# Group 0's lags and the warm-up on all rows, the count tables in step 6, and a new order of the front and the first step

## The reference, cut to what matters

```
ctx    = causal_ema(x, tau_ctx)
gated  = x * sigmoid([x, ctx] @ Wg.T + bg)
h1     = gelu(x @ Wn1.T + bn1)
mod    = 0.5 + sigmoid(h1 @ Wn2.T + bn2)              # 32 values per token
traces = causal_ema(gated * mod[d], tau[d])           # for each of the 32 d
temporal = sum_d traces[d] * softmax(blend)[d]
out    = (gelu(x @ Wsoma.T + bsoma) * sigmoid(temporal @ Wtemp.T + btemp)) @ Wout.T
x      = x + layernorm(out) * gamma + beta

lam    = 10 * exp(-5 * u_prev);   use_sparse = lam >= 1        # per batch
dense  = softmax(q k.T / sqrt(8) + lam * (prior_mask - 1)) v
sparse = softmax over the 32 listed keys of each query, v of the same keys
x      = x + where(use_sparse, sparse, dense) @ Wo.T + bo
```

## Time and profile before

| | us |
|---|---|
| median of three runs (lowest to highest) | 340.48 (339.88 to 341.51) |
| the profiled execution | 342.68 |
| its span in the trace | 340.8 |
| PE busy in the span | 318.4 (93%) |
| DVE | 277.4 (81%) |
| POOL | 246.3 (72%) |
| ACT | 214.9 (63%) |

### The profile page before, as it was taken

The page is one execution under the profiler, slowest core; times in us unless marked ns, Lnnn a source line. Parts: engine busy times, 40 slices in busy tenths (PEclk is TensorE's granted clock), DMA queues, the critical chain, the costliest instruction groups (busy, mean ns, idle before and its releaser), DMA issues. The chain is left out here.

```text
span 340.8 us, 10005 instructions
## 1 busy us (share of the span) xinstructions
PE 318.4 (93%) x3333; PEld 212.4 (62%) x3333; DVE 277.4 (81%) x1453; ACT 214.9 (63%) x458; POOL 246.3 (72%) x298
## 2 busy tenths in 40 slices
PE   7998889999999999989987799999999999999995
PEld 2545355574746556565534576778878777878873
DVE  3895579897888789596788857899999999999982
ACT  5760225555555655644625788788888888888863
POOL 3154266768588676545536777799999999999990
PEclk9996799999999999997999999999999999999999
DMA  6600002023130603210551144565444345401011
GB/s 193 193 3 0 31 0 65 31 68 73 41 100 2 126 14 80 62 32 11 81 82 18 36 90 87 83 109 138 126 102 127 91 127 94 89 4 33 3 33 33
DMA packets 29154, 23.07 MB, mean 68 GB/s; under 512 B 2736, under 2 KB 27824, under 8 KB 29104
## 3 DMA queue, kind: packets, MB, share of 16 engines
q1 hardware_dynamic: 29104, 22.44, 29.0%
HBM read 7.75 MB, written 2.10 MB: 29 GB/s over the span
## 5 line engine op out<-in xcount | busy, mean ns | idle before, releaser
L1593 POOL TENSOR_TENSOR arena<-arena,neg_max 128x512 f32<-128x512 f32 x128 | 129.7, 1042 | 14.0 <-DVE neg_max L1435 13.5
L1435 DVE CUSTOM_DVE_ANT_0 arena<-ps,arena 128x128 f32<-128x128 f32 x512 | 113.7, 286 | 11.2 <-PE ps L765 5.5
L1080 ACT ACTIVATE arena<-ps 128x512 f32<-128x512 f32 x128 | 69.5, 596 | 9.1 <-PE ps L779 9.0
L779 PE MATMUL ps<-ident_sb,arena 128*128 128x128 f32 x512 | 68.2, 276 | 0.0
L1512 POOL TENSOR_TENSOR arena<-arena 128x448 f32<-128x448 f32 (+6 forms) x56 | 42.4, 757 | 31.2 <-DVE arena L1270 27.8
L779 PEld LDWEIGHTS ps<-ident_sb,arena 128*128 128x128 f32 x512 | 56.4, 141 | 7.0 <-issue 4.7
L1435 DVE DVE_READ_ACCUMULATOR2_ANT neg_max<- 128x1 f32 x512 | 42.4, 83 | 0.1
L795 PE MATMUL ps<-arena 128*32 128x128 f32 x1024 | 41.2, 279 | 0.0
L1499 POOL TENSOR_TENSOR arena<-decay_a,arena 128x192 f32<-128x192 f32 x32 | 19.4, 635 | 25.3 <-ACT arena L924 25.3
L1270 DVE SCALAR_TENSOR_TENSOR arena<-ps,lag_c,arena 128x448 f32<-128x448 f32 (+6 forms) x56 | 25.8, 484 | 8.5 <-POOL arena L1512 6.6
L795 PEld LDWEIGHTS ps<-arena 128*32 128x32 f32 x1024 | 24.1, 109 | 6.9 <-issue 0.3
(11 more groups left out here) (168 smaller groups left out, 594.3 us busy)
## 6 DMA issues: line engine op xcount, KB each, us to landing
arena<-q_parts SPq DMA_DIRECT2D x96, 64.0 KB
arena<-k_parts SPq DMA_DIRECT2D x96, 64.0 KB
arena<-in_x SPq DMA_DIRECT2D x16, 256.0 KB, 3.4
arena<-in_xt SPq DMA_DIRECT2D x8, 256.0 KB, 2.8
out<-arena SPq DMA_DIRECT2D x7, 256.0 KB, 3.0
arena<-in_consts SPq DMA_DIRECT2D x1, 420.0 KB, 3.9
w_sb<-in_w SPq DMA_DIRECT2D x1, 384.0 KB, 5.5
w_sb<-in_w SPq DMA_DIRECT2D x1, 192.0 KB, 4.2
```

Of the source, the lines that this page charges most:

```text
L779: mm = pe.transpose(ps[1][:, q % 2, k * P:k * P + P], neg_t[q % NT_RING][:, k * P:k * P + P], ident)
L1080: act.activation(probT[q % PT_RING], ps[1][:, q % 2, :], ACT.Exp, scale=-1.0)\
L1435: dve.tensor_tensor_reduce(out=neg_t[q % NT_RING][:, cs], in0=ps[0][:, score_bank(c) + slot, cs], in1=nbias[n % 2], scale=1.0, scalar=3.0e ...
L1593: pool.tensor_tensor(t4, t4, neg_max[:, n % 2, 4 * z:4 * z + 4].unsqueeze(2).broadcast_to([P, 4, P]), ALU.subtract).then_inc(s["shifted"], 1)
```

## The change

Group 0's lags use all four copies of the modulation with weights divided by four (`NJ`), and so all 128 rows; the bf16 tables for the other groups multiply the four back in. The warm-up at line 412 is 12 matmuls on 128 rows in place of 10 on 64. The `late_tables` move from the end of step 5 to step 6, between lag 1 and `b_temporal`. In the front TensorE does group 1's context at the end, and its `f_gate_x` and the value bias later; VectorE makes only the scaled weights there, splits group 1's modulation, and takes the last carry behind lag 7. In step 0 TensorE does both halves of the gate before `b_cross`, ScalarE the gate's tanh before the copy of the cross sums, and VectorE the tables that left the front.

```diff
-            for _ in range(10):
-                pe.matmul(bank(1, 3), mod_pb[0][0:64, 0:P], mod_pb[0][0:64, :], start=True, stop=True)
+            for _ in range(12):
+                pe.matmul(bank(1, 3), mod_pb[0][:, 0:P], mod_pb[0][:], start=True, stop=True)
...
-                        pe.matmul(bank(u, lag % 2), w_lag[0:D, lag, :], thd[u][0:D, :], start=True, stop=True)\
+                        pe.matmul(bank(u, lag % 2), w_lag[:, lag, :], thd[u], start=True, stop=True)\
...
@@ tensor, front
                 f_lags(i, m, range(2, 4))
+                b_carries(i, m)
+                f_lags(i, m, range(4, 6))
                 f_soma(i, m + 1)
-                b_carries(i, m)
-                f_lags(i, m, range(4, 5))
-                f_gate_x(i, m + 1)
-                f_lags(i, m, range(5, 6))
-                value_bias()
                 f_lags(i, m, range(6, Q))
+                f_context(i, m + 1)
@@ tensor, step
                 if not closes:
                     f_modulation_n(i, m + 1)
-                    f_context(i, m + 1)
+                    f_gate_x(i, m + 1)
+                    f_gate_ctx(i, m + 1)
                     b_cross(i, m)
-                    f_gate_ctx(i, m + 1)
...
                 b_gate(i, m)
+                if not closes:
+                    value_bias()
@@ scalar, step
                 if not closes:
+                    f_context(i, m + 1)
                     f_modulation_n(i, m + 1)
-                    f_context(i, m + 1)
+                    f_gate(i, m + 1)
                     b_cross(i, m)
-                    f_gate(i, m + 1)
@@ vector, constants
-            pro("w_lag", dve.scalar_tensor_tensor(w_lag, half_bw[:].unsqueeze(1).broadcast_to([P, Q, P]), 0.5,
+            pro("w_lag", dve.scalar_tensor_tensor(w_lag, half_bw[:].unsqueeze(1).broadcast_to([P, Q, P]), 0.5 / NJ,
...
-                pro("w_a", dve.tensor_copy(lag_a[:], w_lag))
-                pro("w_rest", dve.tensor_tensor(w_rest, w_lag, lag_a[:], ALU.subtract))
+                pro("w_a", dve.tensor_scalar(lag_a[:], w_lag, float(NJ), None, ALU.mult))
+                pro("w_rest", dve.scalar_tensor_tensor(w_rest, w_lag, float(NJ), lag_a[:], ALU.mult, ALU.subtract))
@@ vector, front
-                early_tables()
+                out_weights()
                 f_lags(i, m, range(2, 4))
-                neighbours()
-                b_carries(i, m)
+                b_carries(i, m, 1, NJ - 1)
                 f_lags(i, m, range(4, 6))
-                dve.wait_ge(s["const_ps"], 2)
-                dve.wait_ge(s["rows_loaded"], 16)
-                pro("kept_bias", ...)
+                dve.wait_ge(s["act_step"], scal("w_a3"))
+                f_mod_parts(i, m + 1)
                 f_lags(i, m, range(6, Q))
-
-                dve.wait_ge(s["act_step"], scal("w_a3"))
+                b_carries(i, m, NJ - 1, NJ)
@@ vector, step
                 if not closes:
-                    f_mod_parts(i, m + 1)
+                    row_factors()
                 f_gated(i, m + 1)
                 f_lags(i, m + 1, range(0, 2))
                 if first < last:
                     counts(first)
+                if 2 * i + m == COUNTED:
+                    late_tables()
                 b_temporal(i, m)
                 f_lags(i, m + 1, range(2, 4))
                 if first < last:
                     counts(first + 1)
+                if not closes:
+                    key_tables()
                 b_mixed(i, m)
                 f_lags(i, m + 1, range(4, 7))
+                if not closes:
+                    dve.wait_ge(s["const_ps"], 2)
+                    dve.wait_ge(s["rows_loaded"], 16)
+                    pro("kept_bias", ...)
+                    neighbours()
                 c_moments(i, m)
                 f_lags(i, m + 1, range(7, Q))
                 c_centre(i, m)
-                if 2 * i + m == COUNTED - 1:
-                    late_tables()
```

More of the change, by code:

```diff
@@ L71 @@
              "blend_4", "lt", "half_bw", "w_lag", "decay_p", "decay_a", "lag_c", "w_a", "w_rest", "w_mid", "w_b2",
-             "w_out", "w_q", "minus_ident_b", "not_prior", "lam", "use", "not_use", "dense_lam",
-             "key_no", "idx_f", "mask_f", "idx_plus", "idx_masked", "kept_bias"] + \
+             "w_out", "w_q", "lam", "use", "not_use", "dense_lam",
+             "key_no", "minus_ident_b", "not_prior", "kept_bias", "idx_f", "mask_f", "idx_plus", "idx_masked"] + \
             [f"hot{r}" for r in range(K_SPARSE // 4)] + ["two_counts", "count", "cnt_one", "cnt_none"]
@@ L436, in f_context @@
                     pe.wait_ge(s["modT_tanh"], grp(i, m, 1, 1))
-                if at_start(i, m, 2) and not at_start(i, m, 1):
-                    pe.wait_ge(s["modn_ready"], 2)
                 four(ctx_bank(i, m), lambda cs: xn[u][:, cs], lambda cs: lt[:], "ctx_ps")
@@ L491, in f_modulation_n @@
                 pe.wait_ge(s["modT_tanh"], grp(i, m, 1, 1))
-                if not at_start(i, m, 2) or at_start(i, m, 1):
-                    pe.wait_ge(s["ctx_ready"], grp(i, m, 1, 1))
+                pe.wait_ge(s["ctx_ready"], grp(i, m, 1, 1))
                 pe.sem_inc(s["modn_begun"], 1)
@@ L1001, in front @@
                 f_mod_part1b(i, m + 1)
+                f_soma(i, m + 1)
             def step(i, m):
@@ L1135, in pro @@
                     dve.wait_ge(s["vec_step"], count[0])
-            for n in range(2):
-                dve.memset(mod_pb[n][0:64, :], 0.0).then_inc(s["half_set"], 1)
+            dve.memset(mod_pb[0][:], 0.0).then_inc(s["half_set"], 1)
+            dve.memset(mod_pb[1][0:64, :], 0.0).then_inc(s["half_set"], 1)
             dve.memset(lag_b[0:64], 0.0).then_inc(s["half_set"], 1)
@@ L1212, in early_tables, with key_tables @@
                 pro("dense_lam", dve.tensor_tensor(dense_lam[:], not_use, lam, ALU.mult), waited=False)
+            def key_tables():
+                dve.wait_ge(s["ident_loaded"], 16)
+                pro("key_no", dve.tensor_copy(key_no[:], c_sb[:, C_K:C_K + P]), waited=False)
+                pro("minus_ident_b", dve.tensor_scalar(minus_ident_b[:], ident, -1.0, None, ALU.mult), waited=False)
+                pro("not_prior", dve.tensor_scalar(not_prior[:], masks_sb[:, 0:P], -1.0, 1.0, ALU.mult, ALU.add))
             def counts(r):
@@ L1275, in each_row_of, with b_carries @@
                 return half_bw[rows_of, :].unsqueeze(1).broadcast_to([rows_of.stop - rows_of.start, GB, P])
-            def b_carries(i, m):
+            def b_carries(i, m, first=1, last=NJ):
                 u = m % 2
                 dve.wait_ge(s["carry_ps"], grp(i, m, 1, 1))
-                for j in range(1, NJ):
+                for j in range(first, last):
                     rows_of = slice((j - 1) * D, j * D)
```

22 lines of the change are left out of this document (8 added, 14 removed).

## The result

| | before | after |
|---|---|---|
| median, us | 341.0 (339.88 to 345.82, 4 runs) | 332.2 (332.14 to 333.14, 4 runs) |
| profiled execution | 342.68 | 332.17 |
| its span | 340.8 | 330.4 |

The ratio is 0.9757, with a 95% interval of 0.9729 to 0.9785: 2.4% faster; it leaves out the slow run of before at 345.82, without which its median is 340.48. Forecast were 332.3 us, 330.0 to 336.0.

What follows compares the result with a forecast made beforehand. The bound was one chain of front and steps before the attention, with TensorE and VectorE awaiting each other. Terms of -7.35, +1.2, -1.6, -1.35 and +0.1 gave -9.0: 333.7 us profiled, 332.3 timed, range 330.0 to 336.0.

Steps and rivals of the forecast that it cites:

- All rows: Group 0's lags in the front: widening to 128 rows costs nothing and removes the first slow clock stretch, from 27.9 us.
- The first rival: Front: the clock falls all the same, since it follows how busy TensorE is; 3.55 us not gained, 335.8; chance 0.14.
- The warm-up: Start of the kernel: with the clock full by 9.8 us, the matmul of line 455 ends earlier, minus 0.3 us.
- The front's tail: From 14.8 us to step 0's local sums: less TensorE work and fewer waits, minus 2.6 us, of which 0.95 is clock.
- one of the signs that the prediction had named against itself: End of the front: the forecast is wrong if VectorE's last carry ends well behind the context.
- Step 0 to the gated input: Step 0 to group 1's gated input: local sums minus 0.9 us, gate beside VectorE's multiplications minus 3.85, of which 1.7 is clock.
- What step 0 takes back: Rest of step 0: moved tables and value bias delay VectorE and TensorE, plus 1.2 us, between 0.6 and 4.0.
- Steps 5 and 6: Moved count tables: wait ahead of step 6's local sums minus 1.6 us, slow stretch minus 1.35, tables in step 6 plus 0.1.
- The other rivals: Among them, VectorE becomes the bound in step 0 through table contention or a slower bf16 table: 333.5 to 335.1 us, chance 0.14.
- the slower case: Step 0's tables make VectorE late, the clock falls at step 1's cross sums for several steps: near 346 us, chance 0.02.
- the one in which nothing moves: The front's gain is lost at a later wait, such as a transfer of the stacks: within 0.5%, chance 0.03.

Runs made afterwards that it cites:

- the split version: Kernel after, with VectorE's three operations on the parts of group 1's modulation spread ahead of lag 6, ahead of lag 7 and behind the last carry: 331.56 us.
- first experiment: Kernel after with group 0's lags on 32 rows again, with the weights of before: 332.48 us.
- a later version: Kernel after with the modulation's parts split and tables moved out of step 0, list and key tables to step 1, batch factors to step 5: 330.68 us.
- wide lags alone: Kernel before with group 0's lags on 128 rows, weights divided by four and the last carry behind lag 7: 338.14 us.
- order alone: Kernel after with lags on 32 rows, the old warm-up and the count tables back at the end of step 5: 337.19 us.
- tables back: Kernel after with the count tables back at the end of step 5: 334.39 us.

## Why the prediction was right, and where it was not

The time was right to 0.1 us, and that is luck: two misses of opposite sign cancel. On the profiled execution the sum said 333.7 and 332.17 came, a gain of 10.5 for the 9.0 of the sum. For the timed runs I took 0.8 of the 2.2 us by which the profiled execution of before lies above them off the gain, and all 2.2 had to go: it was 8.3, from 340.5 to 332.2. The runs of before in the experiments have a clock of 0.976 to 0.990, most of them 0.983 and more, and the profiled one 0.98 with two slow stretches. Of the 1.5 us that the sum lacked, 0.5 is a transfer that landed earlier in this execution. The range held with either number.

**All rows: the step that failed.** "What they may bring is the clock" named the right effect and gave it to the wrong edit. With narrow lags the kernel after keeps the clock and loses 0.3 us; TensorE's old order costs that kernel another 6.3, and its clock. In the order of before the wide lags would have been enough by themselves (2.4 us). The first rival, that the clock falls all the same, did not come. It read the clock from how busy TensorE is, and the runs answer it in two parts. Width does count: with wide lags 1.98 busy of 3.40 us kept the clock that 2.69 of 3.40 with narrow ones had lost. But what the rival had against itself, that the waits ahead of the fall go too, was enough without the width. The sum priced the order as work and waits, and gave it no part in the clock.

**The warm-up: mis-sized.** The term was 0.3; undoing it costs 1.4 in the median and 1.8 in the trace. I read it from one start, in which the second matmul happened to run at the full clock for part of its time. In the trace with the old warm-up and the new order the clock is full only from 12.5 us on.

**The front's tail: size right, by two errors.** 2.6 was predicted; 3.3 came, 0.5 of it from an earlier first transfer (VectorE's first copy at 4.06 against 4.56). At the first lags of group 0, before and after, the lead is 1.0:

```profile
15.04 1.96 PE L527 MATMUL ps<-arena 32*128 32x512 f32 x4
...
14.02 1.98 PE L524 MATMUL ps<-arena 128*128 128x512 f32 x4
```

From there to the local sums it grows by 2.3, the number of the sum. But that VectorE's last carry ends with the context was wrong by a wait of 1.04 us on TensorE, one of the signs that the prediction had named against itself; the split version took 0.7 of it. And "the wider lags cost nothing" was too cautious by as much: with them TensorE is done with the front 1.05 us earlier than with narrow ones (first experiment).

**Step 0 to the gated input: right**, 4.75 against 4.9. Line 1240 follows at once behind the factors of the batches.

**What step 0 takes back: 0.8 for 1.2.** `key_tables` cost 0.1: one of three met a GpSimd addition (0.75 at line 1209), and the idle time held it. The list tables cost about 0.7. Of the twelve operations that moved into step 0 three took longer than their free time: 0.37 at line 1202 (0.17 in before), 0.75 at line 1209 (0.21 at line 1210, the same size) and 0.49 at line 1196 (0.19 free in step 1 of a later version). Each began while a GpSimd addition ran and ended within 0.1 us of that addition's end. This agrees with the rule of the Trainium skill ("SBUF — State Buffer", section "Who interferes with whom") that I set beside this term; what it does not give is how many would meet one, three of twelve and not all. That these tables are on the path is shown by the version without them, 0.9 us faster in the median and 0.6 in the trace.

**Steps 5 and 6: right in the traces.** 1.6 for the wait and 1.35 for the slow stretch came as the sum had them, and the tables cost nothing in step 6. But the slow stretch does not always follow the wait: three traces with it (wide lags alone, order alone, tables back) have no slow stretch in step 6. So 1.35 was a property of the profiled execution, which the slowest runs of before may share (their clock is as low).

**The other rivals.** VectorE was late, by 1.04 in the front, but in step 0 it took back less than forecast, and the bf16 table of the lags, now a multiplication, takes 0.69 us as before (lines 1185 and 1182); the slower case and the one in which nothing moves have nothing in the traces for them.

Open: why single runs took 338.71, 340.38 and 340.67 at clocks that don't account for it; what the pause of TensorE in the attention is; why the same wait lets the clock fall in some executions and not in others; and whether the order holds the clock by filling the waits alone or also by the width of what fills them.

## What to carry to other kernels

Where TensorE's clock falls, look at both the waits and the width of the work ahead of the fall, and try both cures by themselves: wider operands, or work of the next tile placed where TensorE would wait. One of them can be enough, and a fast kernel that has both tells nothing of which it was. Let a window that is read for the cause of a fall end at the fall: the one from 20 to 27 us above stops 0.7 us short of it and shows nothing of the wait. Read a term of the clock from several runs, since its place and length differ from run to run, and line two traces up along the whole span before a difference at the end is put down to the edit. Put tables that nobody waits for into the idle time of a later step.

## What was not expected of the hardware

With f32 matmuls on 32 rows the granted clock fell to 0.5 behind a stretch in which TensorE was busy for 2.69 of 3.40 us; with the same matmuls on 128 rows it stayed full over one with 1.98 of 3.40. Two lags, f32 matmuls of 512 columns, take 1.89 to 1.91 us from start to next start at the full clock on 32 rows and 1.72 to 1.82 on 128 rows: the narrow ones are slower. Twelve warm-up matmuls on 128 rows of zeros had the clock full from 3.8 to 6.8 us on, ten on 64 rows only from 10.3 to 13.2. And one and the same wait of 1.7 us, in the same place of 14 traces, let the clock fall in three.
